# A decoder layer on one core: the scores of keys 64-127 by queries 0-63 are left out, and the orders and engines are laid out anew

## The reference

```
q, k, v = x Wq, x Wk, x Wv (+ biases);  16 heads of 16 channels, 4 key/value heads
q, k = rope(rms_norm(q)) * gain, rope(rms_norm(k))
attn = softmax(where(causal, q k^T / 4, -inf));  f1 = (attn v) Wo + bo
f2 = wkv(time_decay, time_first, x, context)     # a recurrence over the 128 tokens
f3 = relu(x sign(up)^T * up_scale) sign(down)^T * down_scale * output_scale   # 1024 hidden
```

## Time and profile before

| | |
|---|---|
| median of 3 runs | 179.06 us (178.32 to 180.08) |
| profiled execution | span 178.1 us from first to last instruction; the page gives no other time of it |
| PE, DVE busy | 157.8 us, 156.5 us |
| ACT, POOL busy | 138.9 us, 83.4 us |
| chain that ended last | PE 48%, DVE 27%, ACT 10%, issue 8%, DMA 3% |

### The profile page before, as it was taken

How to read it: one execution, slowest core, us unless ns; L and a number is a source line. 1 busy time by engine, 2 the same in 40 slices (tenths; PEclk the granted TensorE clock), 3 DMA queues, 4 the chain that set the end, 5 groups by cost and what they waited for, 6 DMA issues and landing times.

```text
span 178.1 us, 3837 instructions
## 1 busy us (share of the span) xinstructions
PE 157.8 (89%) x1388; PEld 107.8 (61%) x1388; DVE 156.5 (88%) x289; ACT 138.9 (78%) x280; POOL 83.4 (47%) x109
## 2 busy tenths in 40 slices
PE   7978769989999999999999999999969798999920
PEld 2445424545645645566886668769758687898810
DVE  1489679798789999999899999999999999999981
ACT  3745488988998889999899989696687897898700
POOL 8282601017404695020873623699679457270121
PEclk9999969999999999999999999999999999999995
DMA  5899039044709107941070310000300010001122
GB/s 175 244 320 392 5 62 209 2 92 75 249 0 95 56 2 94 212 127 48 0 151 0 75 48 2 0 4 0 118 0 4 0 59 0 36 27 61 63 79 107
DMA packets 17989, 14.65 MB, mean 82 GB/s; under 512 B 12656, under 2 KB 13616, under 8 KB 17712
## 3 DMA queue, kind: packets, MB, share of 16 engines
q1 hardware_dynamic: 17424, 13.87, 29.8%
q10 hardware_dynamic: 544, 0.50, 0.9%
HBM read 9.52 MB, written 2.10 MB: 65 GB/s over the span
## 4 chain that ended last, share of the span: by engine, by line
PE 48%; DVE 27%; ACT 10%; issue 8%; DMA 3%; POOL 2%; SPq 0%; POOLq 0%; DVEq 0%; ACTq 0%
PE banks L417 9%; PE banks L576 8%; PE banks L500 7%; PE banks L597 6%; PE banks L533 5%; DVE hid_lo L1760 5%; DVE state L1702 4%; PE banks L472 4%; ACT probs L971 3%; DMA probs<-biases_dram 3%; DVE ratio L1712 2%; DVE stats L1676 2%; PE banks L510 2%; ACT dn_sb L918 2%; PE banks L479 2%
## 5 line engine op out<-in xcount | busy, mean ns | idle before, releaser
L971 ACT ACTIVATE probs<-banks 128x1024 f32<-128x1024 f32 x32 | 31.8, 1022 | 4.8 <-PE banks L479 4.8
L597 PE MATMUL banks<-dn_sb,hid_hi 128*128 128x256 bf16 x128 | 29.1, 272 | 1.1 <-DVE hid_lo L1760 1.1
L576 PE MATMUL banks<-x2hi,up_sb 128*128 128x256 f16 x128 | 29.1, 273 | 0.8 <-DVE x2lo L1753 0.5
L597 PE MATMUL banks<-dn_sb,hid_lo 128*128 128x256 bf16 x128 | 29.1, 273 | 0.0
L576 PE MATMUL banks<-x2lo,up_sb 128*128 128x256 f16 x128 | 29.0, 272 | 0.0
L417 PE MATMUL banks<-wqkv_sb,xT_sb 128*128 128x384 f32 x64 | 23.5, 512 | 2.0 <-issue 1.6
L1355 POOL TENSOR_SCALAR veps<-stats 128x2 f32<-128x2 f32 x24 | 9.4, 394 | 27.8 <-DVE stats L1676 26.8
L1361 POOL TENSOR_TENSOR rstd<-veps,half_neg 128x2 f32<-128x2 f32 x24 | 20.4, 853 | 1.3
L1019 ACT ACTIVATE banks<-banks,ups_man 128x256 f32<-128x256 f32 x48 | 19.6, 470 | 1.8 <-PE banks L576 1.6
L417 PEld LDWEIGHTS banks<-wqkv_sb,xT_sb 128*128 128x128 f32 x64 | 12.4, 201 | 11.9 <-issue 3.4
L1702 DVE TENSOR_TENSOR_SCAN state<-dec_sb,ke 128x1032 f32<-128x1032 f32 x8 | 18.4, 2301 | 0.0
(11 more groups left out here) (129 smaller groups left out, 355.8 us busy)
## 6 DMA issues: line engine op xcount, KB each, us to landing
ctxT_sb<-ctxT_dram SPq DMA_DIRECT2D x8, 256.0 KB, 3.1
x_sb<-x_dram SPq DMA_DIRECT2D x8, 256.0 KB, 3.8
out_dram<-outb SPq DMA_DIRECT2D x8, 256.0 KB, 2.2
xT_sb<-xT_dram SPq DMA_DIRECT2D x7, 256.0 KB, 4.4
up_f<-up_dram SPq DMA_DIRECT2D x1, 1024.0 KB, 6.4
dn_f<-down_dram SPq DMA_DIRECT2D x1, 1024.0 KB, 8.4
wqkv_sb<-wqkv_dram ACTq DMA_DIRECT2D x2, 192.0 KB, 3.1
xT_sb<-xT_dram SPq DMA_DIRECT2D x2, 128.0 KB, 2.9
```

The source lines that it names most:

```text
L576: mm = nc.tensor.matmul(banks[:, UP[p][n], s * T * S:(s + 1) * T * S], up_sb[:, c, j * 128:(j + 1) * 128], part[:, c, :, :].rearrange("p t ...
L597: mm = nc.tensor.matmul(banks[:, DN[p], t * D:(t + 1) * D], part[:, t * S:(t + 1) * S], down_of(j), start=(j == 0 and t == 0 and m == 0), ...
L971: nc.scalar.activation(probs[:, (T * p + t) % PROBS_N, 2 * h:2 * h + 2].rearrange("p n j s -> p n (j s)"), banks[:, b:b + 2], ACT.Exp).the ...
```

## The change

The scores of keys 64 to 127 by queries 0 to 63 are no longer computed. `scores(p, 0)` makes, for sequence 0, all keys by queries 64 to 127 (256 columns of each bank, `upper`), and for both sequences keys 0 to 63 by queries 0 to 63 (the other 256 columns, `lower`): sequence 0 on partitions 0 to 63, sequence 1 on partitions 64 to 127. `scores(p, 1)` makes sequence 1's upper part in the first halves of four neighbouring banks. `exps` runs three times a pair instead of four, each 128 x 1024. `products` is cut to match, with a copy of sequence 1's first 64 values on partitions 64 to 127 (`v_first`, a second instruction of `take_values`). `probs` has two buffers of a pair, before three of a sequence.

Around it the lists of all engines are written anew, and the bank tables. Of 24 `normed` 18 are on ScalarE after, eight before, each with its `offsets`; 11 of 32 `high_bits` go to POOL (`HID` says which hidden parts lie in SBUF); `low_heads` is all on POOL, most `den_by_rec` on VectorE. The biases come as three rows into a cleared tile and are split on VectorE alone. `gain_in` is loaded from SP. VectorE branches once, ahead of `from_heads`. TensorE projects pairs 0 to 3 ahead of its branch; then come `first_rows`, `project(4)`, `scores(0, 0)`, `scores(0, 1)`, `products(0, 0)`. In POOL's list `high_bits` (2, 0), (2, 3), (4, 2) and (5, 3) stand behind waits on `dn_mm`. The last pair's down projection, scale, sum and store go in halves by sequence. The high and low f16 parts of the third layer's input are held in two buffers (`x2T`), ordered by sequence first; the path `X2_BY_DMA` is off for all pairs.

```diff
-        PROBS_N = 3
+        PROBS_N = 2
...
-        later = sb("later", [128, 4, S], BF16)
+        later = sb("later", [128, 2, S], BF16)
+        early = sb("early", [128, 2, S], BF16)
...
-        probs = sb("probs", [128, PROBS_N, KVH, REP, S])
+        probs = sb("probs", [128, PROBS_N, KVH, 2, REP, HALF])
+        probs_last = sb("probs_last", [128, PROBS_N, KVH, REP, HALF])
...
-            probs_done=4, un_out=2, prec_done=1, att_done=1, attT_out=1,
+            probs_done=3, un_out=2, prec_done=1, att_done=1, attT_out=1,
...
+            guess_done="VGVGGVVV",
+            hi0_done="AGGAAAAG",
+            hi1_done="AAAGAAAG",
+            hi2_done="AAAGGAGA",
+            hi3_done="AAGAAGAG",
+            hi_done="GGGGGGGA",
+            kv_done="VGVVVGVG",
+            lo0_done="VVGGVVVV",
+            lo1_done="VVVVVVVG",
+            lo2_done="VVGVVVVV",
+            lo3_done="GVVVGGVV",
+            newt_done="VVVGVVGV",
+            out_done="AAAVAAAV",
+            qn_done="GGVGGVVG",
+            r3_done="GGVGVGVV",
+            stack_done="AVAAAAVA",
+            x1_done="VAAVAAAA",
+            x2_done="VAAAAAAV")
...
+        SA = ((2, 4), (0, 2), (2, 4), (4, 0), (2, 6), (4, 2), (4, 6), (6, 4))
+        SB = (0, 2, 2, 0, 2, 2, 2, 0)
...
+        NORM_ON_ACT = ((0, 1, 1, 0, 1, 1, 1, 1), (0, 1, 1, 1, 1, 1, 1, 0), (1, 1, 1, 0, 1, 1, 1, 0))
+        HID = ((0, -1, 0, 1), (0, 1, -1, -1), (0, -1, 0, 1), (1, 0, 1, -1), (-1, -1, 1, 0), (-1, -1, -1, 1), (-1, -1, 1, -1), (0, 1, -1, 0))
...
+            def store_half(p, t):
+
+                done(sp, "out_done", p, t + 1)
+                sp.dma_start(out[p][:, t], outb[:, p % OUT_N, t]).then_inc(last_stored, 16)
...
+            sp.wait_ge(bias_clear, 1)
+            sp.dma_start(bias_in[0:BR:32], biases.partition_broadcast(3)).then_inc(bias_in_done, 16)
+            for dst, src in gain_loads:
+                sp.dma_start(dst, src).then_inc(gains_in, 16)
...
+            def block_parts(p, t, tiles, keys, queries, start):
+
                 q = rows[:, p % ROWS_N]
                 for k, kb in enumerate((HB * t + REP, T * HB + t)):
                     for g in range(KVH):
                         r = VW * g
+                        nc.tensor.matmul(tiles[g], q[r:r + VW, kb, keys], q[r:r + VW, HB * t:HB * t + REP, queries],
+                                         start=(start and k == 0), stop=False)
+
+            def mask_parts(tiles, table, last):
+
+                for h in range(2):
                     for g in range(KVH):
                         r = VW * g
+                        mm = nc.tensor.matmul(tiles[g][:, :, h * QTR:(h + 1) * QTR], table[r:r + VW, h, :], masked[r:r + VW],
+                                              start=False, stop=(last and h == 1))
+                        if last and h == 1:
+                            mm.then_inc(sems["scores_mm"], 1)
+
...
+            def scores(p, t, guarded):
+
+                rows_there(p)
+                if p == 0 and t == 0:
+                    pe.wait_ge(masks_ready, MASKS)
+                    pe.wait_ge(guard_ready, GUARDS)
+                first, second = slice(0, HALF), slice(HALF, S)
+                if t == 0:
+                    b = (SA[p][0], SA[p][0] + 1, SA[p][1], SA[p][1] + 1)
+                else:
+                    b = range(SB[p], SB[p] + KVH)
+                upper = [banks[:, x, 0:REP * HALF].rearrange("p (j s) -> p j s", j=REP) for x in b]
+                block_parts(p, t, upper, slice(0, S), second, True)
+                mask_parts(upper, later, t == 1 and not guarded)
+                if t == 0:
+                    lower = [banks[:, x, REP * HALF:2 * REP * HALF].rearrange("p (j s) -> p j s", j=REP) for x in b]
+                    mask_parts(lower, early, False)
+                    q = rows[:, p % ROWS_N]
+                    for k in range(2):
+                        for u in range(T):
+                            kb = (HB * u + REP, T * HB + u)[k]
+                            for g in range(KVH):
+                                r = VW * g
+                                mm = nc.tensor.matmul(lower[g][u * HALF:(u + 1) * HALF], q[r:r + VW, kb, first],
+                                                      q[r:r + VW, HB * u:HB * u + REP, first],
+                                                      start=False, stop=(k == 1 and not guarded))
+                                if k == 1 and u == T - 1 and not guarded:
+                                    mm.then_inc(sems["scores_mm"], 1)
...
-                done(pe, "probs_done", p, 2 * (t + 1))
+                done(pe, "probs_done", p, t + 2)
                 if t == 0:
                     done(pe, "v_out", p)
                     if p == 0:
-                        pe.wait_ge(value_ready, 1)
-                for g in range(KVH):
-                    r = VW * g
-                    nc.tensor.matmul(banks[r:r + VW, PV[p][t], :], v_sb[:, p % V_N, t, g, :],
-                                     probs[:, (T * p + t) % PROBS_N, g].rearrange("p j s -> p (j s)"),
-                                     start=True, stop=True).then_inc(sems["pv_mm"], 1)
+                        pe.wait_ge(value_ready, 2)
+                first, second = slice(0, HALF), slice(HALF, S)
+                to = [[banks[VW * g:VW * g + VW, PV[p][u], :].rearrange("p (j s) -> p j s", j=REP) for g in range(KVH)]
+                      for u in range(T)]
+                if t == 0:
+                    whole = probs[:, p % PROBS_N]
+                    for g in range(KVH):
+                        nc.tensor.matmul(to[0][g][:, :, second], v_sb[:, p % V_N, 0, g, :], whole[:, g, 0], start=True, stop=False)
+                    for u in range(T):
+                        k = slice(u * HALF, (u + 1) * HALF)
+                        for g in range(KVH):
+                            values = v_first[k, p % V_N, g, :] if u else v_sb[k, p % V_N, 0, g, :]
+                            mm = nc.tensor.matmul(to[u][g][:, :, first], values, whole[k, g, 1], start=(u == 1), stop=(u == 0))
+                            if u:
+                                mm.then_inc(sems["pv_mm"], 1)
+                else:
+                    for g in range(KVH):
+                        nc.tensor.matmul(to[1][g][:, :, second], v_sb[:, p % V_N, 1, g, :], probs_last[:, p % PROBS_N, g],
+                                         start=False, stop=True).then_inc(sems["pv_mm"], 1)
...
+            def ffn_down_half(p, t):
+
+                n = NJ // 2 - 1
+                hidden_there(p, n)
+                for s in range(2):
+                    j = 2 * n + s
+                    for m, part in enumerate((hid_hi, hid_lo)):
+                        mm = nc.tensor.matmul(down_tile(p, t), part[:, j, t * S:(t + 1) * S], dn_sb[:, j],
+                                              start=False, stop=(s == 1 and m == 1))
+                mm.then_inc(sems["dn_mm"], 1)
...
-            pe.wait_ge(masks_ready, MASKS)
-            pe.wait_ge(guard_ready, GUARDS)
+            project(2)
+            project(3)
             pe.wait_ge(gain_ready, GAINS)
             plain = pe.value_load(flags[0:1, 0:1], min_val=0, max_val=1)
 
             def from_scores(guarded):
 
-                project(2)
-                done(pe, "rot_done", 0)
-                project(3)
...
+                nc.scalar.activation(v_first[HALF:S, p % V_N, :, 0:HD],
+                                     banks[0:HALF, PJ[p] + 1, QK:E].rearrange("p (g d) -> p g d", g=KVH),
                                      ACT.Copy).then_inc(sems["v_out"], 1)
...
+            def exps(p, k):
+
+                if k < 2:
+                    done(act, "scores_mm", p, KVH)
+                    nc.scalar.activation(probs[:, p % PROBS_N, 2 * k:2 * k + 2].rearrange("p g h j s -> p g (h j s)"),
+                                         banks[:, SA[p][k]:SA[p][k] + 2], ACT.Exp).then_inc(sems["probs_done"], 1)
+                else:
+                    done(act, "scores_mm", p)
+                    nc.scalar.activation(probs_last[:, p % PROBS_N].rearrange("p g j s -> p g (j s)"),
+                                         banks[:, SB[p]:SB[p] + KVH, 0:REP * HALF], ACT.Exp).then_inc(sems["probs_done"], 1)
...
+            def high_bits(p, n):
+
+                done(pool, "hid_done", p, 2 * n + 2)
+                nc.gpsimd.tensor_copy(hid_hi[:, 2 * n:2 * n + 2], hidden(p, n)).then_inc(signal(f"hi{n}_done", p), 1)
...
+            done(pool, "dn_mm", 1, 1)
+            high_bits(2, 0)
+            low_bits(2, 0)
...
+            def scale_half(p, t):
+
+                done(dve, "dn_mm", p, NJ // 2 + t)
+                nc.vector.tensor_tensor(down_tile(p, t), down_tile(p, t), dsc_b[:], ALU.mult).then_inc(sems["o3_done"], 1)
+
+            def add_half(p, t):
+
+                done(dve, "o3_done", p, t + 1)
+                nc.vector.tensor_tensor(r3[:, p % R3_N, t], down_tile(p, t), x2[:, p % X2_N, t], ALU.add)\
```

(28 more changed lines are left out.)

1338 lines of the change are left out of this document (639 added, 699 removed).

## The result

| | before | after |
|---|---|---|
| median of 4 runs | 178.69 us | 185.38 us |
| ratio, 95% interval | | 1.0351 [1.0291, 1.0412] |
| profiled execution, its span | 178.1 us | 185.45 us, 183.7 us |

A forecast was written before the change was run, and what follows sets the result against it. No engine was taken as full from 9 to 104 us, VectorE as the bound to 151, TensorE busy to 170.5. Start -2.4, middle -2.0, stretch -3.0, tail -1.3 gave -8.7: 179.1 to 170.4 us, range 165.5 to 176.5.

The forecast's parts named there:

- POOL costed at nothing: POOL's queue: +7 us of work on an engine 47% busy, and new waits on it, taken to cost no time.
- the slower rival: POOL's 11 casts come out late, each keeping VectorE and TensorE waiting 1.2 us: +13.2 us, 183.6 us; chance 8%.
- The estimate of 177.0 us: By the SBUF exclusion rule alone, casts meeting VectorE operations with two SBUF inputs cost 6.6 us, giving 177.0 us.
- The VectorE sum, -4.9 us: VectorE's work over the whole kernel, operations counted over both orders: 4.9 us less.
- The check under the sum: Whole kernel: VectorE would lose 1.2 us of its idle time beyond its shed work, held to be possible.
- The rival of shapes that don't overlap: Scores and products: 64-row and 64-column tiles run one after the other, +0.12 us a pair, 173.3 us; chance 15%.
- Middle, -2.0: 9 to 104 us: TensorE sheds 3.0 us, VectorE 1.3, neither full; gain between these, taken as 2.0 us.
- 104 to 151 us, -3.0: Stretch where VectorE is the bound: it sheds 3.4 us, TensorE then level with it; gain taken as 3.0 us.
- 151 to 170.5 us, 0: Stretch where TensorE is nearly full: the same feed-forward matmuls, so no change.
- B: GpSimd's queue is too full and its results are late; a rival explanation put to the experiments, without a chance.
- Start, -2.4: Start, up to the first exponentials: earlier biases and filled TensorE waits gain between 0.35 and 4.5 us, taken as 2.4.
- Tail, -1.3: End of the kernel: last pair's scale, sum and store in halves gain between 0.3 and 2 us, taken as 1.3.

The follow-up runs named there:

- experiment 4: Changed kernel with all 32 high halves of the hidden units on ScalarE, the 11 casts leaving GpSimd: 185.14 us, ratio 1.0352.
- experiment 9: Complete changed kernel with nothing but 13 waits added to GpSimd's queue: 177.49 us, ratio 0.9923 to the kernel before.
- experiment 5: Changed kernel with GpSimd's large operations replaced by memsets of their full durations, arithmetic left out: 176.50 us, ratio 0.9860.
- experiment 2: Kernel before with GpSimd's large operations replaced by memsets of about the same time, arithmetic left out: 178.47 us, ratio 0.9978.
- experiments 7 and 16: Kernel before with only the short bias transfer of 3 rows, run twice: 176.87 us and 176.78 us.
- Experiments 3, 8 and 11: 3: kernel before with only the cut, 181.98 us; 8: same, values' second copy read from SBUF, 181.74; 11: experiment 5 plus zero products in scores, 177.33.
- experiment 14: Experiment 9 with the last pair stored as one transfer instead of two halves: 177.64 us, ratio 0.9920.

## Why the prediction was wrong

*POOL costed at nothing, "covered by POOL's idle half"*: this step failed, and with it the 8% that I gave the slower rival. I asked whether GpSimd had time, when the question was whom it stops while it works. The rival was there, tied to the wrong operations: 11 casts at 1.2 us each. That its 183.6 us came near the 185.38 measured is luck. Beside the casts stand 1.3 of the 13.1 us of excess, and experiment 4 shows that without them the loss is the same. What had to be counted was on VectorE's side too: 11 low halves with an SBUF input where there were 3, 18 offsets where there were 8, and mixes put right behind scans, where the GpSimd operation that the scan had held up comes first. Every one of these is a target, whatever GpSimd reads at that moment. The estimate of 177.0 us by the rule of the Trainium skill erred in the same way, in what I applied the rule to: I counted casts again. The runs are at 7.9 us (experiment 9) to 8.9 us (experiment 5) for this step.

*The VectorE sum, -4.9 us*: too large by half. The operations were counted rightly, and 0.60 us is their undisturbed price. But with nobody in its way VectorE is busy 152.4 us (experiment 5) where the kernel before, with the same edit, is busy 155.0 (experiment 2): 2.6 less. The bias splits and the clear ahead of them alone cost 2.4 us more, where I had 1.3; the clear took 0.59 us and not 0.3.

*The check under the sum*: wrong. From -8.7 and -4.9 us it follows that VectorE loses 3.8 us of idle time, not 1.2. Span less busy time is 21.6 us before, 22.1 in experiment 9, 22.0 in experiment 5 and 22.6 in experiment 2: without the meetings the new order took no idle time from VectorE. The forecast needed 3.8 us of it, by its terms at the start and at the tail. The short bias transfer alone took 3.8 to 4.2 us (17.4 and 17.8 left in experiments 7 and 16), and the new order, which has it too, did not keep them.

*TensorE's shapes*: right. The rival of shapes that don't overlap is refuted:

```profile
23.14 0.40 PE L504 MATMUL banks<-rows 32*128 32x256 f16 x8 [0.28 <-DVE rows L1691]
23.36 0.28 PE L512 MATMUL banks<-masked,later 32*128 32x128 bf16 x8
23.48 0.28 PE L512 MATMUL banks<-masked,early 32*128 32x128 bf16 x8
23.68 0.42 PE L540 MATMUL banks<-rows 32*64 32x256 f16 x16
...
26.47 0.40 PE L504 MATMUL banks<-rows 32*128 32x256 f16 x8 [2.37 <-DVE rot L1682]
26.70 0.28 PE L512 MATMUL banks<-masked,later 32*128 32x128 bf16 x8
26.91 0.64 PE L566 MATMUL banks<-probs,v_sb 128*32 128x256 f32 x8
27.48 0.42 PE L571 MATMUL banks<-probs,v_sb 64*32 64x256 f32 x4
```

Sixteen 64-column tiles in 0.42 us, eight upper ones every 0.22 us, the upper product 0.57 us to the next shape.

*Middle, -2.0*: wrong independently of the meetings. I added TensorE's saving to the time because neither engine was full. By the scans, experiment 9 gains 2.7 us to the first one (48.07 against 50.73 us) and 2.5 us to the fourth (95.30 against 97.82): nothing in between. Between experiments 2 and 5, both without meetings, the gain even shrinks there, from 3.3 to 1.8 us. Experiments 3, 8 and 11 say why: VectorE, in order, sets the pace there, at 90% busy.

*104 to 151 us, -3.0*: experiment 9 has gained 3.1 us by the fifth scan and 3.6 by the last (136.24 against 139.83), so about -0.5. The orders differ, and another mark gives another lead (4.2 us at the last mix, 2.8 at the last sum ahead of the third layer), so this is good to about 1 us. VectorE has less to do there, but the time did not follow by as much.

*151 to 170.5 us, 0*: in experiment 9 +1.9 us (last scale at 168.81 against 170.49, after a lead of 3.6): the casts and sums on GpSimd are late, VectorE waits 0.76 and 0.33 us for them and 1.38 for a sum. This is what is left of B.

*Start, -2.4*: right in size (2.6 at the first scan), by luck. I gave the short bias transfer 0.35 us, "only that is to be had"; alone it brings the first scan 3.3 us and the time 2.2 us (experiments 7 and 16). I had looked at TensorE's wait for the biases, when VectorE's whole queue stood behind them. The waits that I wanted to fill were not saved: the one of 2.37 us in the rows above, for the rotation of pair 3, is new and stands where the wait for the exponentials was.

*Tail, -1.3*: -0.5. In experiment 9 the last norm follows the last half scale by 2.84 us (before 3.98 from the last scale), but the end is 4.2 us behind it instead of 3.7. Both halves wait for one norm, so halving the store can't help (experiment 14).

Sum by experiment 9: -2.7 + 0.2 - 1.1 + 1.9 - 0.5 = -2.2 us of span (178.1 to 175.9), where I had -8.7; the middle term here runs to the fourth scan and the next from there. The meetings, +7.9 us of median, come on top. Of the 15 us between forecast and result, about half is thus the meetings and the rest gains that did not come. What stays open is the division of the cut's own 0.6 to 2 us, and which waits took up the VectorE time that the new order freed.
